# Row maxima three steps ahead of the exps in place of four, in a fused attention and SwiGLU kernel

## The reference

```python
xn = _layernorm(x, axis=-1)
q = (xn @ Wq.T + bq).reshape(b, t, 16, 8)      # 16 heads of 8, rotary embedding on q and k
k = (xn @ Wk.T + bk).reshape(b, t, 4, 8)       # 4 key/value heads, each used by 4 query heads
v = (xn @ Wv.T + bv).reshape(b, t, 4, 8)
scores = einsum('bthd,bshd->btsh', q, k) / sqrt(8)
probs = softmax(scores, axis=2)
attn = einsum('btsh,bshd->bthd', probs, v).reshape(b, t, 128) @ Wo.T + bo
h = silu(xn @ w_gate') * (xn @ w_up')          # hidden size 384
out = x + attn + h @ w_down'
```

## Time and profile before

| | |
|---|---|
| median of 3 runs | 801.42 us (801.06 to 803.97) |
| profiled execution | 805.1 us, span of the instructions 802.6 us |
| PE, DVE, ACT, POOL busy | 92%, 87%, 76%, 27% of the span |
| mean granted PE clock | 0.971 of full speed |
| DMA | mean 38 GB/s |

### The profile page before, as it was taken

One profiled execution on the slowest core, in us unless ns is written; L12 is line 12 of the kernel. 1 busy time (PEld: TensorE's weight loads), 2 busy tenths in 40 slices (PEclk: granted clock), 3 DMA queues, 4 the chain that ended last, 5 costly groups with the idle time before them and its releaser, 6 DMA issues.

```text
span 802.6 us, 13776 instructions
## 1 busy us (share of the span) xinstructions
PE 735.0 (92%) x4856; PEld 236.9 (30%) x4856; DVE 701.9 (87%) x1268; ACT 613.2 (76%) x1219; POOL 214.6 (27%) x349
## 2 busy tenths in 40 slices
PE   3596999999999999999999999999999999999996
PEld 1221232232232232322322322323232232233353
DVE  6678799999999999999999999999999999999731
ACT  1432688878887888888887878888888888788864
POOL 3238127373641211203030302112030303021210
PEclk9777799999999999999999999999999999999998
DMA  6201212103020111111010101111110101010020
GB/s 212 83 16 36 64 31 68 33 19 82 4 76 23 32 30 32 32 31 31 22 41 7 44 14 31 30 31 31 31 32 27 36 7 50 7 32 1 2 80 26
DMA packets 29204, 30.42 MB, mean 38 GB/s; under 512 B 6673, under 2 KB 21265, under 8 KB 29009
## 3 DMA queue, kind: packets, MB, share of 16 engines
q1 hardware_dynamic: 27552, 25.05, 11.1%
q0 software_dynamic: 720, 2.36, 1.0%
q10 hardware_dynamic: 864, 2.15, 0.7%
HBM read 23.12 MB, written 6.03 MB: 36 GB/s over the span
## 4 chain that ended last, share of the span: by engine, by line
PE 71%; DVE 15%; ACT 9%; issue 2%; DMA 2%; SPq 1%; ACTq 0%; DVEq 0%
PE acc_ps L918 28%; PE banks L832 18%; DVE mx L683 12%; PE banks L849 9%; ACT probs L529 8%; PE banks L924 6%; PE banks L933 3%; PE banks L941 3%; DMA y_all<-in_x 1%; PE banks L958 1%; PE banks L808 1%; PE banks L802 1%; PE banks L949 0%; SPq L299 0%; DMA qa<-q_parts 0%
## 5 line engine op out<-in xcount | busy, mean ns | idle before, releaser
L683 DVE TENSOR_REDUCE mx<-banks 128x1 f32<-128x512 f32 x1024 | 638.2, 684 | 52.6 <-PE banks L832 51.4
L529 ACT ACTIVATE probs<-banks 128x512 f32<-128x512 f32 x1024 | 541.2, 602 | 123.2 <-PE banks L849 122.9
L849 PE MATMUL banks<-qc,kc 51*128 51x512 bf16 x1024 | 307.6, 385 | 23.4 <-ACT probs L529 10.8
L832 PE MATMUL banks<-ka,qa 48*128 48x512 bf16 x1024 | 291.9, 388 | 14.4 <-DVE mx L683 7.2
L918 PE MATMUL acc_ps<-probs,v_grp 128*32 128x512 f32 x2048 | 273.4, 606 | 0.0
L832 PEld LDWEIGHTS banks<-ka,qa 48*128 48x128 bf16 x1024 | 78.0, 94 | 312.6 <-DVE mx L683 227.3
L849 PEld LDWEIGHTS banks<-qc,kc 51*128 51x128 bf16 x1024 | 74.8, 94 | 92.5 <-ACT probs L529 88.1
L417 POOL TENSOR_TENSOR neg_max<-row_max,nought 128x16 bf16<-128x16 f32 x31 | 6.8, 220 | 307.5 <-DVE row_max L689 307.5
L918 PEld LDWEIGHTS acc_ps<-probs,v_grp 128*32 128x32 f32 x2048 | 40.4, 108 | 58.5 <-issue 46.6
L460 POOL TENSOR_TENSOR gated<-gu 128x256 f32<-128x256 f32 x48 | 34.9, 728 | 76.6 <-ACT gu L581 76.6
L924 PE MATMUL banks<-xn_T,w_ffn 128*128 128x256 f32 x192 | 54.8, 409 | 0.0
(11 more groups left out here) (92 smaller groups left out, 291.3 us busy)
## 6 DMA issues: line engine op xcount, KB each, us to landing
qa<-q_parts SPq DMA_DIRECT2D x32, 96.0 KB
qc<-q_parts SPq DMA_DIRECT2D x64, 48.0 KB
q_parts<-part POOLq DMA_DIRECT2D x9, 256.0 KB, 4.1
y_all<-in_x SPq DMA_DIRECT2D x4, 512.0 KB, 12.1
qa<-q_parts SPq DMA_DIRECT2D x32, 64.0 KB
qc<-q_parts SPq DMA_DIRECT2D x64, 32.0 KB
out<-y_all SPq DMA_DIRECT2D x8, 256.0 KB, 2.3
ka<-k_parts SPq DMA_DIRECT2D x32, 48.0 KB
```

The costliest lines, as they stand in the source:

```text
L529: nc.scalar.activation(probs[:, s % SLOTS, j, :], banks[:, score_bank(G * s + j), :], ACT.Exp, scale=SCALE).then_inc(exp_done, 1)
L683: nc.vector.tensor_reduce(out=mx[:, h, col, k:k + 1], in_=ps, op=ALU.max, axis=AX.X).then_inc(max_done, 1)
L832: nc.tensor.matmul(ps, qa[par][rows, j // 2, t * P:(t + 1) * P], ka[par][rows, k * W:(k + 1) * W], start=True, stop=True).then_inc(a_ready, 1)
L849: nc.tensor.matmul(banks[:, score_bank(u), :], kc[par][rows, kt * P:(kt + 1) * P], qc[par][rows, h, j // 2, :], start=True, stop=True).the ...
```

## The change

One constant. `LEAD` goes from 48 to 44, and the tables are left alone:

```diff
--- before.py
+++ after.py
@@ -33,7 +33,7 @@
 HU = G * HT * 2
 AU = NH * HU
 PER = AU // STEPS
-LEAD = 48
+LEAD = 44
 S_BANKS = 3
 RING = 4
 FIRST_RING = 3
```

## The result

The changed kernel takes 833.03 us (median of 4 runs, 829.38 to 834.31) against 801.24 us for the kernel before (4 runs), a ratio of 1.0383 with a 95% interval of 1.034 to 1.0425. That is 31.8 us more. The forecast was 830, with 820 to 841 as its range.

The account below looks back on a forecast made before the run. It took a 2.48 us round of PE and ACT as the bound, with DVE on the path at the transposes; 27.8 + 2.3 - 1.4 = +28.7 us on 801.4 gave 830.1, range 820 to 841.

Parts of the forecast that it names:

- The stall and its place: Steps 5 and 13: the transpose waits for POOL's chain, making the next unit 0.94 and 0.91 us late.
- That it isn't repaid: Steps after each transpose: PE and ACT turn in a 2.48 us round that repays nothing, so the whole 0.94 counts.
- Sum over the groups: Groups 0 to 14, both transposes: 15 x (0.94 + 0.91) = 27.8 us.
- The row maximum: Moving `max_rows` out of steps 3 and 11 gains nothing; in steps 4 and 12 its 0.18 us is on the path.
- The last group: Its one transpose, in step 5, comes 2.3 us later, and all behind it too.
- the fallen clock: Rival: the clock halves for 15.9 us after each of 31 new pauses; +200 us, about 1030; chance 0.02.
- The prologue: Four units fewer let scores start 2.1 us earlier; partly spent at half clock (0.6 of their worth stays), 1.4 us won.
- Absorbed: Rival: PE's spare time repays each stall in the next two steps; 801 us, no change; chance 0.05.
- half absorbed: Rival: each stall in the groups counts 0.5 us; +16 us, 817; chance 0.08.
- Contention of POOL and DVE: Rival: POOL at work slows the moved row maximum by 0.9 us, 31 times; 858 us; chance 0.02.
- The larger stall: Rival: stalls up to the transpose's 1.26 us, or some loads or POOL work also late; 834 to 845 us; chance 0.13.
- What the profile would show: Groups of 45.8 us, 31 PE pauses of some 1.2 us before line 837 released by POOL, first scores near 79.6.

Follow-up runs that it names:

- the two operations more: The changed kernel (LEAD 44) with two more operations of 0.22 us in POOL's chain, which compute nothing new: 860.23 us, ratio 1.0746.
- LEAD 46: The kernel before with the constant LEAD at 46 in place of 48, and the waits tied to it rewritten to hold for it: 804.96 us, ratio 1.0052.
- the single POOL operation: The changed kernel with POOL's chain of four operations in split_max cut to its first: 805.32 us, ratio 1.0058.
- the turned order of that group's jobs: The changed kernel with PROJ and STAGE before the transpose in step 5 of the last group: 829.18 us, ratio 1.0346.
- LEAD 48 with two operations more: The kernel before (LEAD 48) with two more operations of 0.22 us in POOL's chain, which compute nothing new: 800.42 us, ratio 0.9992.

## Why the prediction was right

**The stall and its place.** Right. The transpose came 1.28 us later in its step (forecast 1.26) and the next unit 1.03 us later (forecast 0.94 and 0.91). Three terms of the chain were off. From the transpose to the unit behind it I took 0.09 us from the last group, and it was 604.05 - 603.89 = 0.16. The release of PE after POOL took 0.14 and not 0.05. Against that the four reductions of step 4 took 2.48 us and not 3 x 0.62 + 0.69 = 2.55, since a unit of the train came every 0.60. Together 0.94 + 0.07 + 0.09 - 0.07 = 1.03. The way from the row maximum to the end of POOL's chain held to a hundredth.

**That it isn't repaid.** Right but for 0.11 us in a group (below), shown by the table of steps, and by the two operations more, where the steps with the clock at 1.00 grew by 0.60 for 0.59.

**Sum over the groups.** 27.8 forecast, 29.3 measured. Two stalls of 1.03 for 0.94 and 0.91 are 3.2 us more over the groups, and step 7 gave 0.11 back in each, 1.6 us, which I hadn't foreseen. I had written that step 7 finds the rows of maxima there, which held, but before the change they had been just late. The score at its start came after its unit by 0.07 us in the group of the rows (589.09 and 589.02), by 0.06 to 0.14 over the groups; behind a stall of 1.03 the two start together.

**The row maximum.** I counted its place in steps 4 and 12 within the chain, and said that taking it out of steps 3 and 11 wins nothing. Both held. What I didn't see is that its 0.18 us would count even with POOL's chain covered or cut, as LEAD 46 and the single POOL operation showed.

**The last group.** The term that was mis-sized: 2.3 forecast, 4.0 measured. The transpose came 2.3 us later as worked out, but the pause before it, 2.07 us, brought the clock down, as the turned order of that group's jobs showed, and PROJ, STAGE and `weigh` behind it took longer. I had the fallen clock as a rival for all groups, with 0.02, and dismissed it by a pause of 1.21 us that was of the length of the other thirty, not of this one. In those thirty it stayed at 1.00, as forecast. The Trainium skill, TensorE: Matmul & The Clock Gate, section "A second HAM failure mode: psum-queue depth-cycling", says that frequent short idle times between groups of matmuls can make the clock swing between its levels; the trace agrees for pauses of 1.8 us and more (8 of 30 of 1.81 us in the run with two more operations), and not for the thirty of 1.2.

**The prologue.** 1.4 forecast, 1.5 left over in the sum, but this agreement is partly luck: the interval of the ratio is 3.4 us wide to each side. The first `weigh` stood at 82.29 us in the profile of the changed kernel and at 85.32 in that of before, but at 81.19 in that of LEAD 48 with two operations more, which has the prologue of before. So no run shows what the four units less are worth, nor the share of 0.6 by which I reduced it.

**The rivals.** Absorbed and half absorbed are excluded by the table of steps. Contention of POOL and DVE didn't occur: line 689 took 0.18 us in all of its 31 places in the steps. The larger stall didn't come, within the groups. The fallen clock came once, in the last group.

**What the profile would show.** Groups of 45.9 us for 45.8, pauses of 1.2 us before line 837, L689 at 0.18. The first scores came at 78.9 for 79.6. Wrong was the releaser: the tables and the chain name DVE, and only the single POOL operation showed that it is POOL. Wrong also was that POOL would wait for L689 as long as before: 394.5 us in 31 pieces for 307.5 in 30.

## What to carry to other kernels

The distance between a producer and its consumer has to hold the whole path between them: here row maximum, four small operations on another engine, transpose, copy and DMA. With four steps the slack of this path was spread so that each wait was just covered (the last by some 0.1 us too little); taking one step away put 1.03 us on the path of each half. Moving the transpose moved the wait on to the DMA: behind `weigh`, within the same step, this took about half of the loss away (818 us for 833), a whole step later it made the kernel far slower (927 us). Before such a distance is shortened, walk the path from the last input on, with the durations of the trace, up to the first consumer, and compare it with the step times. A small operation on a nearly full engine is free only where that engine waits anyway; and an order that pairs matmuls on the two row halves of the array has to be kept when a count shifts it.

## What the hardware showed that was not expected

- **Clock.** Pauses of PE of 1.2 us, thirty in the changed kernel, left the clock at 1.00. Of thirty pauses of 1.81 us, in the run with two more operations, 8 were followed by two microseconds or more at 0.50 and 22 were not. The pause of 2.07 us in the last group was; with that pause cut to 0.50 us the clock stayed at 1.00. Two pauses in each group, of 1.7 to 2.2 us, in the run with the transposes at 6 and 14, brought the mean clock to 0.898.
- **Pairing.** A matmul of 48 and one of 51 rows on different row halves start together (584.05 both); on the same half each takes a place of 0.22 us of its own (585.81 and 586.03), 64 us over the kernel.
- **A small DMA.** From the end of ACT's copy (586.27) to the first score that needed the two transfers of 6 KB (589.09), 2.82 us passed in the kernel before.
